# Eight search steps of even and odd head-tiles as two instruction streams with a slot for every step

## The reference, cut to what matters

```python
Q = (x_text @ Wq).reshape(Bb, Tt, H, DH)          # 4 heads of 32
K = (x_vision @ Wk).reshape(Bb, Gg, H, DH)
scores = jnp.einsum('bthd,bghd->bhtg', Q, K) / np.sqrt(DH)
scores = jnp.where(vision_mask[:, None, None, :], scores, -jnp.inf)
topv, topi = jax.lax.top_k(scores, 32)
probs = jax.nn.softmax(topv, axis=-1)
attn = jnp.zeros_like(scores).at[bi, hi, ti, topi].set(probs)
c_t = jnp.einsum('btg,bgd->btd', attn.mean(axis=1), x_vision @ Wv) * text_mask[..., None]
x = layernorm(x_text, g_norm_in, b_norm_in)
scale_in, shift_in = jnp.split(c_t @ W_film_in + b_film_in, 2, axis=-1)
x = x * (1.0 + mod_gate * scale_in) + mod_gate * shift_in
y = s4d(x, ...)                                    # rfft, product with the kernel's spectrum, irfft
...                                                # FiLM out, residual, layer norm, gelu MLP, layer norm
logits = h @ gate_w; top_id = argmax(logits); score = sigmoid(max(logits))
y = rt_down[e]( silu((h*score) @ rt_gate[e]) * ((h*score) @ rt_up[e]) )   # for e = top_id
out = x + tanh(g_ffn) * (shared_swiglu(h) + y)
```

## Time and profile before

| | us |
|---|---|
| median of 3 runs | 1795.5 (1794.97 to 1796.42) |
| span of the profiled execution | 1792.4 |
| PE busy, instructions | 1401.2 (78%), 6243 |
| PE weight loads | 983.5 (55%), 6251 |
| DVE busy | 1484.0 (83%), 2102 |
| ACT busy | 1109.9 (62%), 2362 |
| POOL busy | 1195.8 (67%), 1341 |
| DVE L1422, max on w, 384 | 471.3, 1227 ns each |
| DVE L1425, replace on w, 384 | 464.1, 1209 ns each |
| DVE L1414, max from PSUM, 128 | 156.2, 1221 ns each |
| DVE L1418, replace from PSUM, 128 | 155.5, 1215 ns each |

### The profile page before, as it was taken

One profiled execution on the slowest core, in us unless ns is written; L12 is line 12 of the kernel. 1 busy time (PEld: TensorE's weight loads), 2 busy tenths in 40 slices (PEclk: granted clock), 3 DMA queues, 4 the chain that ended last, 5 costly groups with the idle time before them and its releaser, 6 DMA issues.

```text
span 1792.4 us, 20766 instructions
## 1 busy us (share of the span) xinstructions
PE 1401.2 (78%) x6243; PEld 983.5 (55%) x6251; DVE 1484.0 (83%) x2102; ACT 1109.9 (62%) x2362; POOL 1195.8 (67%) x1341
## 2 busy tenths in 40 slices
PE   5566658778876887688888878887887778887896
PEld 3243435455544554456565647664655465655796
DVE  7999999998999999989998999999998995112221
ACT  3789844866485648565986588657865676134442
POOL 1499838577857785688678966896688668624232
PEclk7666778878887888799998999898989989998998
DMA  7200121012001200213322322233222201663232
GB/s 210 65 4 4 35 53 50 24 34 67 7 24 43 58 15 17 51 46 95 97 55 65 100 76 54 57 86 100 53 57 65 91 16 53 202 194 108 61 51 27
DMA packets 97218, 115.15 MB, mean 64 GB/s; under 512 B 17840, under 2 KB 74168, under 8 KB 96964
## 3 DMA queue, kind: packets, MB, share of 16 engines
q1 hardware_dynamic: 85348, 100.32, 19.2%
q0 software_dynamic: 11760, 13.52, 4.9%
HBM read 75.48 MB, written 19.58 MB: 53 GB/s over the span
## 4 chain that ended last, share of the span: by engine, by line
DVE 57%; PE 14%; issue 10%; POOL 8%; ACT 7%; DMA 2%; SPq 1%; POOLq 0%; DVEq 0%; ACTq 0%
DVE R L1422 20%; DVE ZB L1425 16%; DVE ZB L1418 7%; DVE R L1414 6%; DVE R L1379 2%; ACT ZB L1007 2%; PE PS L1969 2%; DMA out<-R 2%; PE PS L2083 2%; ACT R L1013 2%; POOL ZB L731 1%; PE PS L1991 1%; POOL R L910 1%; PE PS L2056 1%; ACT R L1007 1%
## 5 line engine op out<-in xcount | busy, mean ns | idle before, releaser
L1422 DVE MAX8 R<-ZB 128x8 f32<-128x1024 f32 x384 | 471.3, 1227 | 12.2
L1425 DVE MATCH_REPLACE8 ZB<-R,ZB 128x1024 f32<-128x1024 f32 x384 | 464.1, 1209 | 0.0
L731 POOL TENSOR_TENSOR ZB<-ZB 128x1024 f32<-128x1024 f32 x96 | 231.6, 2412 | 94.9 <-ACT ZB L1007 85.6
L1010 ACT ACTIVATE R<-PS 128x512 f32<-128x512 f32 (+6 forms) x404 | 178.1, 469 | 175.3 <-PE PS L2064 28.7
L733 POOL TENSOR_TENSOR ZB<-ZB 128x1024 f32<-128x1024 f32 x96 | 226.3, 2358 | 7.5
L1007 ACT ACTIVATE R<-R 128x32 f32<-128x32 f32 (+4 forms) x356 | 96.4, 275 | 197.4 <-DVE R L1422 172.1
L1414 DVE MAX8 R<-PS 128x8 f32<-128x1024 f32 x128 | 156.2, 1221 | 1.1 <-PE PS L1720 1.1
L1418 DVE MATCH_REPLACE8 ZB<-R,PS 128x1024 f32<-128x1024 f32 x128 | 155.5, 1215 | 0.0
L1013 ACT ACTIVATE R<-R 128x1 f32<-128x1 f32 (+1 forms) x384 | 140.8, 391 | 20.0 <-POOL R L718 15.3
L1007 ACT ACTIVATE ZB<-ZB,R 128x1024 f32<-128x1024 f32 x128 | 146.3, 1143 | 0.3 <-DVE ZB L1425 0.2
L1007 ACT ACTIVATE ZB<-PS,R 128x1024 f32<-128x1024 f32 x128 | 142.7, 1114 | 4.2
(11 more groups left out here) (248 smaller groups left out, 3030.0 us busy)
## 6 DMA issues: line engine op xcount, KB each, us to landing
ZR<-ZR SPq DMA_DIRECT2D x96, 128.0 KB
ZB<-in_L_ffn_rt_gate SPq DMA_DIRECT2D x21, 512.0 KB, 4.2
ZB<-in_L_ffn_rt_up SPq DMA_DIRECT2D x21, 512.0 KB, 5.0
ZB<-in_L_ffn_rt_down SPq DMA_DIRECT2D x21, 512.0 KB, 6.3
R<-in_x SPq DMA_DIRECT2D x16, 512.0 KB, 4.8
ZB<-in_ctx SPq DMA_DIRECT2D x8, 768.0 KB, 5.2
R<-xs_d SPq DMA_DIRECT2D x39, 128.5 KB, 2.1
out<-R SPq DMA_DIRECT2D x32, 128.0 KB, 2.0
```

The lines of the kernel that those rows point to most:

```text
L731: pool.tensor_tensor(e, e, w, ALU.subtract).then_inc(s.g_att, 1)
L1010: return act.activation(o, i, ACT.Copy, **k)
L1422: vec.max(ml[:, 8 * r:8 * r + 8], w).then_inc(s.v_tk, 1)
L1425: vec.match_replace(w, ml[:, 8 * r:8 * r + 8], w, NEG).then_inc(s.v_tk, 1)
```

## The change

The head-tiles' part on DVE becomes two parts, one for even n and one for odd n. Each takes the slot of every step from a new table `DVE_TOP` (16 head-tiles by 8 steps). The semaphore v_tk becomes two, one for each parity, with 8 (n // 2) in place of 8 n; the waits of ACT and of SP's last loads are rewritten to match. The values in all other slot tables are replaced. No instruction is added, taken away or given another shape.

```diff
-            def attention():
-                for n in range(16 * B):
-                    ml, w = mx[n % 3], tk[n % 2]
-                    yield tile_at(n)
+            def attention(odd):
+                for n in range(odd, 16 * B, 2):
+                    ml, w, at = mx[n % 3], tk[n % 2], DVE_TOP[n % 16]
+                    yield tile_at(n) + at[0]
                     on.wait_ge(s.p_sc, n + 1)
                     on.wait_ge(s.a_att, 7 * (n - 3) + 3)
-                    vec.max(ml[:, 0:8], sc_bank(n)).then_inc(s.v_tk, 1)
-                    yield tile_at(n) + 1
-                    on.wait_ge(s.v_tk, 8 * n + 1)
+                    vec.max(ml[:, 0:8], sc_bank(n)).then_inc(s_tk[n % 2], 1)
+                    yield tile_at(n) + at[1]
+                    on.wait_ge(s_tk[n % 2], 8 * (n // 2) + 1)
                     on.wait_ge(s.g_att, taken(n - 2))
-                    vec.match_replace(w, ml[:, 0:8], sc_bank(n), NEG).then_inc(s.v_tk, 1)
+                    vec.match_replace(w, ml[:, 0:8], sc_bank(n), NEG).then_inc(s_tk[n % 2], 1)
                     for r in range(1, 4):
-                        yield tile_at(n) + 2 * r
-                        on.wait_ge(s.v_tk, 8 * n + 2 * r)
-                        vec.max(ml[:, 8 * r:8 * r + 8], w).then_inc(s.v_tk, 1)
...
-            weave(setup(), attention(), prep(), weights(), kernel_rows(), post(), tiles(), routed())
+            weave(setup(), attention(0), attention(1), prep(), weights(), kernel_rows(), post(), tiles(), routed())
...
+DVE_TOP = ((43.9, -4.1, 47.4, 48.4, 50.3, -99.6, 56.1, 63.3), (40.6, 46.1, 54.6, -243.2, 59.1, -105.3, -138.3, -379.1), (52.7,
+          -194.1, -203.4, -29, -23.7, -69.5, 57.4, 59.2), (48.1, 21, 50.3, -84.4, 51.5, 10.9, 53.6, -60.5), (46.5, 30.4, 50,
...
-DVE_MOMENTS = ((55.7, 111.7), (26, 111.2))
-DVE_ROUTE = ((118.3, 119.4), (123.3, 123.3))
+DVE_MOMENTS = ((97.9, 157.1), (-138.9, 117.9))
+DVE_ROUTE = ((164.2, 165.5), (-42, -142.3))
-ACT_ROOT = ((61, 98.8, 116.1), (35, 70.4, 89.4))
+ACT_ROOT = ((61.2, -131.8, 127.4), (71.8, -649.1, 112))
-ACT_SH = ((134.2, 135, 145.6, 145.6), (134, 134, 138.1, 161.5))
+ACT_SH = ((150.8, -177.1, -1.4, -26.4), (145.6, -63.1, 94.8, 76.7))
-POOL_SH = ((133.7, 135.1, 136.1, 143), (141.9, 147, 148, 148.3))
+POOL_SH = ((231.3, 92.6, 178.9, 169.2), (148.8, 135, -188.7, -230.4))
-ACT_SHUP = ((123.8, 128, 131.3, 132.7), (121.2, 121.2, 126.4, 129.2))
+ACT_SHUP = ((130.8, 140.2, -284.4, 144.6), (119.4, 137.4, -27.8, 82.6))
-PE_PREP = (4, 8.2, 11.8, 14.8, 14.8, 21.6, 39.1, 39.2, 40.3)
+PE_PREP = (-14.4, -14, -3.9, -3.6, -3.4, -1.7, 12.1, 14.4, 17)
-PE_RAY = (-65.7, -21.2, -12.8)
+PE_RAY = (-79.9, -65.1, -14.6)
-SP_TILE = ((-36.8, -3.2, 1.6), (1.6, 3.2, 6.5), (6.7, 6.7, 31.9), (36, 38.5, 42), (69.6, 70.2, 83.9), (-27.4, -9, -7.7), (1.6,
...
+SP_TILE = ((132.5, 78, 86.3), (-519.2, 125.1, -39.2), (81, 111.7, 135.9), (101.6, 53.6, 126.7), (-49, 138.6, -21.4), (11.6,
...
```

More of the change, by code:

```diff
@@ new lines @@
+POOL_FILM_OUT = ((59.3, -133.5, -277.2, -1031.9), (99.7, 102.1, 59.1, 20.6))
+POOL_ROOT = ((119.4, 129.1, 130.3), (118.6, 145.2, 147.3))
+POOL_RESIDUAL = ((121.6, -39.2, -40.6, -113.4), (144, 28.6, 25, -116.8))
+POOL_OUT = ((-490.7, -94.9, -14.6, -1003.8), (86.1, 102.1, 112, -79.1))
+POOL_ROUTE = ((131.8, 101.3, 51), (37.9, 23.7, -140.8))
+POOL_SH = ((231.3, 92.6, 178.9, 169.2), (148.8, 135, -188.7, -230.4))
+POOL_PREP = (66.9, 190.3)
+POOL_LOW = (97.4, 70.4, 74.8)
+ACT_FILM_IN = ((31.9, -25.8, -114, -116.5), (-222.5, -78.7, -156.9, -515.3))
@@ new lines @@
+ACT_INV = ((54.7, -2), (46.4, -79.9))
+ACT_FILM_OUT = ((56.2, -117.5, 40.3, -284.9),)
+ACT_ROOT = ((61.2, -131.8, 127.4), (71.8, -649.1, 112))
+ACT_NORM = ((62.4, 130), (-89.7, -914.4))
+ACT_TURN = ((70.8, -21.4), (10.5, -58))
+ACT_UP = ((78.9, -16.6, -246.3, -57.9, 90.5, -193.5, 94.9, 34), (79.9, 60.7, -353.6, -73.9, 3.3, -282.1, -149.1, -146.1))
+ACT_DOWN = ((102.9, -96, -42.3, 109.5), (5, 68.1, 91.6, -76.7))
+ACT_OUT = ((114.6, 115, -7.5, -48.6), (107.3, 43, -177.1, -264.4))
+ACT_TURN2 = ((-63.7, 60.6), (-0.1, -125.2))
@@ new lines @@
+ACT_ROUTE = ((-928.8, -38.4), (115, 127.6))
+ACT_SILU = ((126.2, 144.5), (-174.1, 126.8))
+ACT_SH = ((150.8, -177.1, -1.4, -26.4), (145.6, -63.1, 94.8, 76.7))
+DVE_SPECTRUM = ((80.5, 82.7, 85.7, 0.7), (54.3, -97.8, -63.8, -316.7))
+DVE_MOMENTS = ((97.9, 157.1), (-138.9, 117.9))
+DVE_ROUTE = ((164.2, 165.5), (-42, -142.3))
+ACT_PREP = (18.8, 21.9, 26.7)
+ACT_QUERY = (34.8, 24.6, 37.6)
+ACT_CONTEXT = (17.7, 56.3)
+ACT_KEY = (24.8, 63.1)
+ACT_FINISH = ((9.6, -87.8, 14, 20.1), (23.2, -95.7, 26.1, 38.5), (15.1, -63.8, 27.7, 30.9), (10.7, -402.4, 13.1, 13.4))
@@ new lines @@
+SP_QUERY = (82.5, -232.7, -410.5, -62.6)
+SP_KEYS = (157.3, -39.9, -393.2, 18.9)
+SP_INPUT = (79.5, 126.7)
+SP_POST = ((138.6, 139.5, -191.5, -443.2, 63.1), (38.9, 78.6, -28.8, 154.6, -83))
+SP_TILE = ((132.5, 78, 86.3), (-519.2, 125.1, -39.2), (81, 111.7, 135.9), (101.6, 53.6, 126.7), (-49, 138.6, -21.4), (11.6,
+          -296.1, -584.8), (18, -80.5, -322.8), (-67.3, 61.7, -288.9), (-334.2, -95.9, -106.5))
+ACT_SHUP = ((130.8, 140.2, -284.4, 144.6), (119.4, 137.4, -27.8, 82.6))
+POOL_SHUP = ((131.9, 132.9, 129.5, 66.1), (147.7, -76.5, -118.7, -134.9))
@@ new lines @@
+ACT_MOMENTS = (5.9, 7.7)
+PE_WEIGHT = (-36.7, -4.7, -1, -0.9, -0.7, 0)
+ACT_WEIGHT = (-189.2, -57.8, -142, 7.9, -40.5)
+DVE_WEIGHT = (15.3,)
+POOL_WEIGHT = (54.6,)
+DVE_RAY = (5.3, -137.9, -60)
+ACT_RAY = (-26.5, -8.6, -24.2)
+PE_RAY = (-79.9, -65.1, -14.6)
+DVE_CHUNK = ((-44.6, 46.6), (58.9, 64.2), (68.9, 79.9), (85.5, 96.4), (97.5, 109), (110.5, 119.7), (132.1, 133.4), (135.7,
+          140.1))
+PE_CHUNK = ((-14.5, -8.8, -4, -0.9, 0.6, 1.5), (-0.3, 0, 0.3, 4.5, 8.1, 9.6), (4.8, 5.8, 9.1, 11.1, 20.2, 21.2), (13.3, 16.9,
+          20.9, 21.3, 33.6, 36.8), (24.1, 29.1, 34.3, 40.2, 43.7, 48), (41, 41.7, 43.2, 45.4, 57, 59.7), (52.9, 54.9, 56.4,
+          58, 63.8, 63.8), (61, 61.6, 62.7, 63.3, 78.6, 79.6))
@@ L214 @@
+SP_CHUNK = (137.5, 123, 93.2, 119.1, 136.9, 211.6, 251.8, 249.9, -461.6)
+SP_LATE = (126.9, 215)
+PE_END = (85.8, 93.6, 108.7, 113.4, 127.2, 127.2)
+ACT_END = (132.1, 139.6, 88.1, -115, 13.1, 107.9)
+DVE_END = (164.5, 169.1, 175.6, 177.9, 188.9, -442.5)
+DVE_FILM_OUT = (-111.9, -46.9, -82.6, -176)
+DVE_DOWN = (77.4, 104.1, -83.4, -138.8)
 T_TURN, T_GATE, T_UP, T_DOWN = range(4)
```

116 lines of the change are left out of this document (37 added, 79 removed), and 14 rows, old and new, of tables (DVE_TOP, POST_AT).

## The result

The changed kernel takes 1814.3 us (median of 4 runs, 1808.9 to 1821.4) against 1796.0: ratio 1.0105, interval 1.0078 to 1.0133. Repeated later on another chip it took 1812.4 against 1797.0: 1.0076 (1.0056 to 1.0096). It is slower by about 1%, where 1772 was forecast with 0.84 for faster.

The account below looks back on a forecast made before the run. DVE's order was taken to bound the eight batches, a chain over ACT, PE, POOL and DMA the tail. Terms -2.2 -5.4 -5.2 -3.0 +2.7 -11.9 = -25.0, 2 added back, gave 1772 us, own range 1765 to 1779.

Parts of the forecast that it names:

- broken pairs: DVE's search steps: 192 neighbouring pairs no longer dependent, 0.12 us saved each, 23 us if every one counts.
- the spectrum's 0.4 us: Batches 4 to 7: DVE reaches its wait at the spectrum's second half one step later, -0.4 us a batch.
- rival 1: DVE's steps: broken pairs save nothing, operand order moves the starts; 1791 us, chance 0.10.
- Rival 3: Head-tile batches: streams leave too little room for a head-tile's second half, DVE waits on POOL's sums; 1805 us, chance 0.10.
- The router's step: Router on DVE: route 0 comes one step earlier, its longer wait takes back 1.1 us a batch (bounds 0 to 1.3).
- Start: Before the first max: PE's key products go ahead of the first angle products, +2.7 us (bounds 0 to +3.5).
- Tail: After the last batch: new orders on four engines remove waits on the chain, -11.9 us in sum.
- the batch's down products: Tail: the last rest-exponential on ACT loses a table load and two copies ahead of it, -1.5 us.
- tile 19's term: Tail: expert tile 19's bank copy precedes root 1 on ACT, removing PE's 5.36 us wait; -2.6 us (0 to -5.4).
- the ranks, the shared expert and the picks: Tail: PE's rank wait filled -1.5 us, shared silu before the copies -1.7, weight picks overlapping down products -1.5.
- the accumulation's 3.1: Tail: the fourth shared output's copy precedes the first routed silu, ending POOL's 23.38 us wait; -3.1 us (0 to -4.7).
- Rival 2: Tail gives nothing: 18 expert weight loads make tiles late or removed waits reappear at the next link; 1784 us, chance 0.16.

Follow-up runs that it names:

- e13: Kernel before, in batches 2 to 7 step 1 of the next head-tile moved ahead of steps 6, 7 and 8: ratio 1.0451, 83 us over the one-step swap.
- e5: Kernel before, in batches 2 to 7 only step 1 of the next head-tile and step 8 of the present one change places: 1795.0 us, 0.9988.
- e1: Kernel before with only the new interleaved order of DVE's eight steps, from head-tile 32 on: 1823.7 us, ratio 1.0149.
- e2: Changed kernel with DVE's order of before, all other engines in the new order: 1844.3 us, ratio 1.0250.
- e3: Changed kernel with the first shared product group behind the ranks again in batches 0 to 6: 1827.1 us, ratio 1.0154.
- e4: Changed kernel with PE's first pieces (mask transpose, angle products, keys) in the old order: 1808.3 us, ratio 1.0060.
- e6: Kernel before with the new orders of all five engines only for the last batch's post part and tiles 17 to 20: 1794.4 us, 0.9987.
- e14: Changed kernel with the one-step swap on DVE instead of the new table from head-tile 32 on: 1864.7 us, ratio 1.0362.
- e12: Kernel before with the one-step swap in batches 2, 3, 5, 6 and 7, not 4, and the new tail: 1787.1 us, 0.9947.
- e8: Changed kernel again with no edit, on another chip: 1812.4 us against 1797.0, ratio 1.0076.

## Why the prediction was wrong, point by point

**The step that failed** is the one that made broken pairs into time: "So 192 pairs are broken, x 0.12 = 23 us if every one counts. They do where DVE waits for nothing." It put new waits at nothing (but for the router's 1.1 us and the spectrum's 0.4 us a batch). The runs showed 48.0 us of new waits between the first max and the last step, 18.0 of them for scores and 16.1 for the router, against the 23 us of the pairs.

DVE hardly waits in the old order because each of its steps also gives the others 1.24 us to bring the next scores. A pair is broken by taking a step of another head-tile forward, and that takes room from the chain step 7, exponential, scores, step 1. I read DVE's idle time (36.6 us of 1447) and took it for slack; it shows that little is late, not by how much the rest is early. The view to read was the distance in steps from each result to its next use, against the queues on the way. e13 against e5 shows this mechanism with the pairs held. e1 against before shows that the new table costs 25 us in the old surroundings, and e2 against before that the other engines' new orders cost 33.5 us with the old steps. In the changed kernel the waits for scores are 18.0 of the 48.0 us; how the rest divides between the table and the other orders is not shown.

**Pairs.** The 0.12 us stood every test. In the changed kernel, DVE's timeline of batch 2's end (a replace behind another head-tile's replace, then a max behind it):

```profile
610.14 0.09 DVE L1437 MATCH_VALUE_LOAD ZB<-R,ZB 128x8 f32 x1
...
611.35 0.08 DVE L1437 MATCH_VALUE_LOAD ZB<-R,ZB 128x8 f32 x1
...
612.54 1.22 DVE L1434 MAX8 R<-ZB 128x8 f32<-128x1024 f32 x1
613.79 0.09 DVE L1437 MATCH_VALUE_LOAD ZB<-R,ZB 128x8 f32 x1
```

610.14 to 611.35 is 1.21, 611.35 to 612.54 is 1.19 and 612.54 to 613.79, a replace behind its own max, 1.25. Over the span the medians of the changed trace are 1.321 for a max behind its own replace and 1.204 for one behind another's. So rival 1 is out. The rule of the Trainium skill beside it ("VectorE: DVE Perf Modes", The DRAIN you can't avoid) is that the next operation starts only when the pipe is empty, with or without a semaphore; for these two operations the trace disagrees by 0.12 us. The section also says that a next operation that is not held starts earlier, which the prediction left out.

**Rival 3** was the right kind and badly priced. I gave it 0.10 and looked at step 8, POOL's sum and step 2; the link that failed is step 7, the exponential, the scores and step 1. I had computed "at the least 6.2 us against 3.5 of work", the bare chain, with one piece of other work in the way. In e13 there were two copies and a table load on ACT, and 6.7 us of groups on PE. The sign that the prediction had named for this rival, waits on POOL's sums in number, did come (24 against 7), but at 19.5 against 16.8 us they cost little.

**The router's step** was priced rightly: route 0's wait went from 2.13 to 3.40 us, +1.27, for +1.1 forecast. The rank wait, 1.24 to 3.14, was overlooked, although I had used the same move of a shared group as a gain in the tail. Over the seven batches the two grew by 9.3 and 6.8 us. The ranks' part was not worth the 13 us that e3 expected: e3 handed it on.

**Start.** +2.7 forecast, bounds 0 to 3.5; the first angle copy came 4.4 us late and the first max 5.1. I had one cause. The mask's transpose also stands behind the context now, and DVE waits for it ahead of its moments (the copies of the changed kernel that answer to the earlier trace rows, and PE's first angle products, to the earlier trace rows):

```profile
12.30 0.19 DVE L1418 COPY R<-PS 128x32 f32<-128x32 f32 x1 [6.25 <-PE PS L1718]
...
18.41 1.61 DVE L1477 COPY R<-PS 128x256 f32<-128x256 f32 x4 [4.06 <-PE PS L1841]
```

```profile
10.06 1.11 PE L1771 MATMUL PS<-R,ZB 128*128 128x128 f32 x4 [10.06 <-DMA ZB<-in_ctx]
...
13.28 2.04 PE L1783 MATMUL PS<-R,ZB 128*128 128x512 f32 x2 [1.01 <-ACT R L1022]
15.26 2.07 PE L1784 MATMUL PS<-R,ZB 64*128 64x512 f32 x2
17.26 1.97 PE L1841 MATMUL PS<-R 128*128 128x128 f32 x8
```

The key products took 2.04 and 2.07 us, not 1.09 each, though the granted clock was 1.00 in both traces; why is open. Of batch 0's +9.6, waits for angle chunks and for scores are what the list shows (3.6 us each at 80.66 and 137.70); e4 leaves it, and which entry makes it is open.

**Tail.** -6.1 of -11.9, and e6 shows it as a gain by itself. The milestones, in us after the last search step, before and changed: the batch's down products end at 105.0 and 103.3 (forecast -1.5, measured -1.6); the second turn ends at 133.3 and 133.2; the ranks start at 137.7 and 140.8, the first routed products at 169.6 and 166.8, the last scatter at 274.8 and 269.3. Of tile 19's term (-2.6) nothing arrived at the second turn. The 5.36 us ahead of its first products are gone, and 32 of them take 3.73 us where they took 6.04; but 4.43 us (0.96 before) now stand ahead of its down products, which take 3.75 us at a granted clock of 0.50 (1.97 at 1.00 before), and 6.41 us for ACT (1.92 before) ahead of the second turn. PE's rows of the changed kernel, to be read against the earlier trace rows:

```profile
1647.41 3.75 PE L2076 MATMUL PS<-ZB,R 128*128 128x256 f32 x8 [4.43 <-issue]
...
1667.27 1.97 PE L1970 MATMUL PS<-R 128*128 128x128 f32 x8 [6.41 <-ACT R L1025]
...
1673.43 3.64 PE L2041 MATMUL PS<-R 128*128 128x512 f32 x4
1676.90 0.30 PE L2017 MATMUL PS<-R 128*128 128x32 f32 x2
...
1693.67 7.15 PE L2049 MATMUL PS<-R 128*128 128x256 f32 x24 [3.24 <-POOL R L916]
```

The ranks wait for nothing now but stand behind 3.64 us of shared products instead of 1.4 us of idle time; the shared part's wait is 3.24 (3.74). From the second turn to the first routed products 2.8 us were gained, where the ranks, the shared expert and the picks had been priced at 4.7 together; which of the three fell short is not shown. From there to the last scatter it is 2.7, close to the accumulation's 3.1: the copies are early and POOL's 23.38 us wait is gone, with the tile scatters in its place.

```profile
1698.02 0.99 POOL L907 DMA_DIRECT2D out<-R  x1 [4.40 <-ACT R L1022]
...
1706.69 1.74 POOL L907 DMA_DIRECT2D out<-R  x2 [5.98 <-DMA out<-R]
...
1717.63 1.54 POOL L997 DMA_INDIRECT out<-R  x1 [2.97 <-DMA out<-R]
```

Rival 2's expert loads made nothing later: PE's only wait for a load from 1536 us on is 1.8 us for one expert's up weights, where before it was 2.2.

## What to carry to other kernels

An engine that never waits in the profile isn't thereby free to be reordered: count, for each buffer that goes round, the steps between the last use of its content and the next need of it, and see what stands in the queues on the way. In this kernel a tenth of a microsecond a step, gained by taking steps forward, was eaten at once by waits: with a single step taken forward it broke even (e5), with three it cost 83 us (e13). Orders of several engines that were made together lost when they were mixed (e1, e2, e14); e12 came from keeping what had paid in one stretch and leaving the rest.

## What the runs showed of the hardware

Two executions of the same changed kernel differ at one place of the start. The 32 products of the weight rows in PE's timeline, in the first profile and in e8's:

```profile
51.37 3.73 PE L1812 MATMUL PS<-R 128*128 128x1 f32 x32
```

```profile
52.70 6.99 PE L1812 MATMUL PS<-R 128*128 128x1 f32 x32
```

3.73 us at one time and 6.99 at the other. The granted clock was 1.00 from 51.4 to 55.1 us in the first and 0.50 from 52.7 to 59.7 us in the second, the two levels of TensorE's clock, 2.4 and 1.2 GHz; in both PE had idled more than 15 us up to 44 us. The first max came at 65.0 and at 70.0. The kernel before has the same group (6.99 us in its trace), but DVE is busy until its first max and doesn't wait for it. So the clock at one place can move the first max by 5 us once DVE waits for PE there. The runs of the changed kernel spread over 14 us, those of the old one over 6. This place alone doesn't explain it: e4, whose first max comes at 58.8 although its group takes 6.83 us, spreads over 14 us too. That the rest comes from other places where DVE now waits for PE is a guess that no run tests.
